# Last stage of a graph kernel: the scalar edge attribute moved into a second one-hot, edge weights formed two pairs ahead, ScalarE without its products of the weights

## What is computed

```python
tpw = h @ W_mlp4 / sqrt(64)
w1, w2, w3, w4 = split(tpw, 4)                 # 128 each
p1 = w1 * s0 * y0
p2 = (w2 * s0)[:, :, None] * y1[:, None, :]
p3 = w3[:, :, None] * s1 * y0[:, None, :]
p4 = w4 * einsum('eum,em->eu', s1, y1) / sqrt(3)
msg0 = segment_sum(concat(p1, p4), receiver)   # target node
msg1 = segment_sum(concat(p2, p3), receiver)
out = x1 + linear(msg0, msg1) / 10             # x1: the node features before this layer
```

## Time and profile before

| | |
|---|---|
| runs | 5696.2, 5701.41, 5704.77 us |
| profiled execution | 5664.33 us, span 5662.4 us |
| mean granted TensorE clock | 0.938 of full; 0.99 from 3191 us on |
| TensorE busy | 4809.4 us (85%), weight loads 2243.0 |
| VectorE busy | 2867.7 us (51%) |
| ScalarE busy | 2291.3 us (40%) |
| GpSimd busy | 2726.7 us (48%) |
| last stage, 3191 to 5663 us | TensorE 2279.0, VectorE 1782.5, ScalarE 1547.9, GpSimd 928.7 us busy |

### The profile page before, as it was taken

The page is one execution under the profiler, slowest core; times in us unless marked ns, Lnnn a source line. Parts: engine busy times, 40 slices in busy tenths (PEclk is TensorE's granted clock), DMA queues, the critical chain, the costliest instruction groups (busy, mean ns, idle before and its releaser), DMA issues.

```text
span 5662.4 us, 106923 instructions
## 1 busy us (share of the span) xinstructions
PE 4809.4 (85%) x17040; PEld 2243.0 (40%) x17041; DVE 2867.7 (51%) x8231; ACT 2291.3 (40%) x6164; POOL 2726.7 (48%) x3492
## 2 busy tenths in 40 slices
PE   7898566778898878887788899999999999998998
PEld 5443122333343223333344444444444444444444
DVE  7543122334453111123344577777777777777676
ACT  0442000111112223431223466666666666666565
POOL 0333666776664655456666344433333333333332
PEclk9998677899998889998899999999999999999999
DMA  2233666777776767667777444444433343333333
GB/s 83 95 106 112 178 191 205 222 227 234 238 246 191 214 207 220 195 208 236 249 254 267 148 119 115 116 116 118 120 112 115 117 120 113 115 117 113 113 117 95
DMA packets 433675, 916.83 MB, mean 162 GB/s; under 512 B 63093, under 2 KB 170869, under 8 KB 433510
## 3 DMA queue, kind: packets, MB, share of 16 engines
q0 software_dynamic: 195840, 641.89, 38.0%
q1 hardware_dynamic: 182918, 245.65, 13.0%
q10 hardware_dynamic: 54880, 28.91, 1.7%
HBM read 787.79 MB, written 128.41 MB: 162 GB/s over the span
## 4 chain that ended last, share of the span: by engine, by line
PE 30%; issue 24%; DVE 11%; DVEq 8%; ACT 7%; ACTq 7%; POOL 4%; DMA 3%; another core or an unknown queue 3%; POOLq 2%; SPq 0%
PE bank L1267 8%; POOL ring L544 4%; PE bank L1392 3%; PE bank L1223 3%; PE bank L1225 3%; ACT hB L788 3%; ACTq L785 3%; ACT dense_w L799 3%; DVEq L1110 2%; DVE hA L1118 2%; DVE hA L1104 2%; DVEq L1120 2%; DMA ef<-in_ef_t_dram 2%; PE bank L1310 2%
## 5 line engine op out<-in xcount | busy, mean ns | idle before, releaser
L544 POOL DMA_INDIRECT ring<-tab_d,idx x1568 | 1549.7, 988 | 817.4 <-issue 523.2
L1392 PE MATMUL bank<-dense_w,oh 128*128 128x512 f32 x3520 | 1618.6, 602 | 71.2 <-DVE dense_w L1127 70.3
L1267 PE MATMUL bank<-ring,ohp 128*128 x3904 | 1105.4, 436 | 462.0 <-POOLq L556 226.2
L510 POOL DMA_INDIRECT ring<-up_d,idx x880 | 856.7, 973 | 498.5 <-POOL idx L506 348.4
L799 ACT ACTIVATE dense_w<-hA,hC 128x128 f32<-128x128 f32 x2640 | 820.0, 389 | 664.4 <-DVE hA L1118 599.5
L1392 PEld LDWEIGHTS bank<-dense_w,oh 128*128 128x128 f32 x3520 | 632.8, 189 | 863.0 <-issue 666.7
L1267 PEld LDWEIGHTS bank<-ring,ohp 128*128 x3904 | 411.3, 107 | 1134.2 <-issue 866.0
L1015 DVE TENSOR_TENSOR ohp<-iota_w,dst_f 128x512 f32 x392 | 266.5, 692 | 679.8 <-PE bank L1267 246.3
L506 POOL COPY idx<-src_i 128x2 int32 x440 | 80.5, 183 | 1054.3 <-DVE dense_w L1127 1012.2
L1382 PE MATMUL bank<-w,hC 64*128 64x256 f32 x3520 | 504.6, 404 | 31.5 <-issue 20.9
L1104 DVE SCALAR_TENSOR_TENSOR hA<-ring,hC,hB 128x128 f32<-128x128 f32 x880 | 270.9, 349 | 500.9 <-ACT hB L788 436.6
(11 more groups left out here) (180 smaller groups left out, 4917.6 us busy)
## 6 DMA issues: line engine op xcount, KB each, us to landing
hC<-hid_d SPq DMA_DIRECT2D x440, 64.0 KB
tab_d<-tout SPq DMA_DIRECT2D x98, 256.0 KB, 2.8
tw<-tab_d SPq DMA_DIRECT2D x98, 256.0 KB
hlw<-hl_d SPq DMA_DIRECT2D x98, 256.0 KB
ring<-tab_d,idx POOLq DMA_INDIRECT x1568
hid_d<-hC ACTq DMA_DIRECT2D x98, 256.0 KB
hl_d<-agg SPq DMA_DIRECT2D x74, 256.0 KB, 3.1
ring<-up_d,idx POOLq DMA_INDIRECT x880
```

The costliest lines, as they stand in the source:

```text
L510: g_.indirect_dma_start(ring_v[:, b, k, :], None, table, bass.IndirectOffsetOnAxis(idx_t[:, b, k:k + 1], 0)).then_inc(S["got"][b], 16)
L544: g_.indirect_dma_start(ring_h[:, b, k, :], None, table, bass.IndirectOffsetOnAxis(idx_b[:, b, k:k + 1], 0)).then_inc(S["got"][b], 16)
L1267: ins = pe.matmul(bank[0][:, :], ohp_b[:, bass.ds(at, 1), k, :].rearrange("p b n -> p (b n)"), ring_b[:, bass.ds(slot, 1), k, h, :].rearra ...
L1392: ins = pe.matmul(bank[h][:, :], oh[:, b, k, :], msg[:, b, k, h, :], start=False, stop=False, skip_group_check=True)
```

## The change

- y0 is no longer multiplied into the weights. The one-hot for h = 0 is a second one, `oh0`, whose entries are y0 in place of 1: one `tensor_scalar` per tile with two operations (equal, then times y0), both with a scalar operand from memory. ScalarE's w13 products (L793) go, with their semaphores `w13` and `w_read`.
- The weights are two products of 512 columns per pair, into two adjacent banks, and there are two sets of these banks. The weights of pair n + 2 follow the sums of pair n.
- VectorE's order in a pair becomes: one-hot, t2 (one instruction for both tiles), p1 (one for both), wait for q0, q1, drain, q2, p3 (read from PSUM), the two weighted one-hots, drain, p4 (one for both). t2 has two buffers.
- The closing touches go; the copies of banks 0 and 1 wait for the last sum's `seg_done`. The second pair of a window is taken out of the loop, and the copy to `mT` comes behind it; the output product comes after the window's second sum.
- A window has at least `MINV` = 4 pairs in place of 2.

```diff
-        bank = [ctx.enter_context(nc.psum_tensor(f"bank{i}", [P, D], F32)) for i in range(8)]
+        ps = ctx.enter_context(nc.psum_tensor("bank", [P, 8, D], F32))
+        bank = [ps[:, i, :] for i in range(8)]
...
-        w_bank = [[bank[2], bank[3]], [bank[7], bank[5]]]
-        m_bank = [bank[4], bank[6]]
+        w_bank = [ps[:, 2:4, :], ps[:, 4:6, :]]
+        m_bank = [bank[6], bank[7]]
...
 weigh (ScalarE):
-                    ac.wait_ge(M["w_done"], n + 2)
-                    ac.wait_ge(M["u_used"], n + (NU - 1))
-                    for k in range(2):
-                        ins = ac.mul(w13[:, k, :], w_bank[k][0][:, 0:2 * P], yg[:, b, 4 * k:4 * k + 1])
-                    ins.then_inc(M["w13"], 1)
...
 messages (VectorE):
+                    w = w_bank[b]
+                    ve.wait_ge(M["seg_done"], n)
+                    ve.tensor_tensor(oh[:, b, :, :], iota_w[:, :].unsqueeze(1).broadcast_to([P, 2, P]),
+                                     dst_f[:, bass.ds(g * 2, 2)].unsqueeze(2).broadcast_to([P, 2, P]), ALU.is_equal)
+                    ve.wait_ge(M["got"][ub], ve.snap((n + (NU - 1)) // NU * 32))
+                    ve.wait_ge(M["w_done"], n + 2)
+                    ve.tensor_tensor(t2[:, b, :, :], w[:, :, 2 * P:3 * P], u[:, :, 0:P], ALU.mult).then_inc(M["t2"], 1)
+                    ve.tensor_tensor(msg[:, b, :, 0, 0:P], w[:, :, 0:P], u[:, :, 0:P], ALU.mult)
                     ve.wait_ge(M["q0"], n)
                     (q1, two instructions, as before)
-                    ve.wait_ge(M["seg_done"], n)
-                    (the one-hot)
                     ve.drain()
                     (q2, two instructions, as before)
-                    (t2, drain, p4, wait for w13, p1 and p3: eight instructions)
+                    for k in range(2):
+                        ve.tensor_tensor(msg[:, b, k, 0, P:].rearrange("p (m u) -> p m u", m=3),
+                                         w[:, k, P:2 * P].unsqueeze(1).broadcast_to([P, 3, P]),
+                                         u[:, k, P:4 * P].rearrange("p (m u) -> p m u", m=3), ALU.mult)
+                    for k in range(2):
+                        ve.tensor_scalar(oh0[:, b, k, :], iota_w[:, :], dst_f[:, bass.ds(g * 2 + k, 1)],
+                                         yg[:, b, 4 * k:4 * k + 1], ALU.is_equal, ALU.mult)
+                    ve.drain()
+                    ve.tensor_tensor(msg[:, b, :, 1, 0:P], q2[:, :, :], w[:, :, 3 * P:4 * P], ALU.mult).then_inc(M["u_used"], 1)
...
 window (ScalarE and VectorE; finish on VectorE only):
+                second_pair(w)
+                if not isinstance(w, int) or w > 0:
+                    copy_mT(w - 1)
                 rest(w)
                 if not isinstance(w, int) or w > 0:
                     finish(w - 1)
                 if not isinstance(w, int) or w < NW - 1:
                     first_pair(w + 1)
                 keep_b(w)
-                copy_mT(w)
...
 edge_weights and sum_pair (TensorE):
-                pe.wait_ge(M["w_read"], n)
-                pe.wait_ge(M["w13"], n)
-                for h in range(2):
-                    for k in range(2):
-                        ins = pe.matmul(w_bank[k][h][:, 0:2 * P], hid[k * HID:(k + 1) * HID, b, :],
-                                        w4[k * HID:(k + 1) * HID, h * 2 * P:(h + 1) * 2 * P], start=True, stop=True)
+                if not isinstance(n, int):
+                    pe.wait_ge(M["u_used"], n + (NU - 2))
+                for k in range(2):
+                    ins = pe.matmul(w_bank[b][:, k, :], hid[k * HID:(k + 1) * HID, b, :],
+                                    w4[k * HID:(k + 1) * HID, :], start=True, stop=True)
...
-                        ins = pe.matmul(bank[h][:, :], oh[:, b, k, :], msg[:, b, k, h, :], start=False, stop=False,
-                                        skip_group_check=True)
+                        ins = pe.matmul(bank[h][:, :], (oh0, oh)[h][:, b, k, :], msg[:, b, k, h, :], start=False,
+                                        stop=(last and k == 1), skip_group_check=True)
...
 the loop (TensorE):
+                def one(b):
+                    sum_pair(n, b, last)
+                    if ahead:
+                        edge_weights(n + 2, b)
...
+                step(True)
+                if not isinstance(w, int) or w < NW - 1:
+                    step(True)
+                    if not isinstance(w, int) or w > 0:
+                        out_product(w - 1)
+                    with pe.Fori(lo + 2, hi - 1) as g:
+                        step(True)
+                    step(True, True)
...
-                touch(bank[0][:, :], D, False)
-                touch(bank[1][:, :], D, False).then_inc(M["sum_done"], 1)
```

More of the change, by code:

```diff
@@ L32 @@
 LAG = 1
+MINV = 4
 NU = 4
@@ L176, in build @@
         yg = hC[:, 1, 0:16].rearrange("p (b n) -> p b n", b=2)
-        w13 = hA[:, 0, :].rearrange("p (k n) -> p k n", k=2)
-        t2, q1 = (hA[:, 1, i * 256:(i + 1) * 256].rearrange("p (k n) -> p k n", k=2) for i in range(2))
+        t2 = hA[:, 0, :].rearrange("p (b k n) -> p b k n", b=2, k=2)
+        q1 = hA[:, 1, 0:256].rearrange("p (k n) -> p k n", k=2)
+        oh0 = yb[:, :].rearrange("p (b k n) -> p b k n", b=2, k=2)
         q2 = hB[:, 0, 0:256].rearrange("p (k n) -> p k n", k=2)
@@ L809, in first_pair, with second_pair @@
                 weigh(lo)
+            def second_pair(w):
+                weigh(ac.snap(lo_r) + 1)
             def rest(w):
-                with ac.Fori(ac.snap(lo_r) + 1, ac.snap(hi_r)) as g:
+                with ac.Fori(ac.snap(lo_r) + 2, ac.snap(hi_r)) as g:
                     weigh(g)
             def keep_a(w):
-                ac.wait_ge(M["sum_done"], w + 1)
+                more = 1 if isinstance(w, int) and w == NW - 1 else 0
+                ac.wait_ge(M["seg_done"], ac.snap(c) + more)
                 after(ac, M["turned"], w)
@@ L893, in _ @@
             ve.drain()
-            ve.tensor_scalar(rcol[:, 0:1], rcol[:, 6:7], float(NG - 2), None, ALU.min)
+            ve.tensor_scalar(rcol[:, 0:1], rcol[:, 6:7], float(NG - MINV), None, ALU.min)
             ve.tensor_reduce(rcol[:, 5:6], rtmp2[:, :], X, ALU.max)
             ve.drain()
-            ve.scalar_tensor_tensor(out=rcol[:, 1:2], in0=rcol[:, 0:1], scalar=2.0, in1=rcol[:, 5:6],
+            ve.scalar_tensor_tensor(out=rcol[:, 1:2], in0=rcol[:, 0:1], scalar=float(MINV), in1=rcol[:, 5:6],
                                     op0=ALU.add, op1=ALU.max)
@@ L1138, in first_pair, with second_pair @@
                 messages(lo)
+            def second_pair(w):
+                messages(ve.snap(lo_r) + 1)
             def rest(w):
-                with ve.Fori(ve.snap(lo_r) + 1, ve.snap(hi_r)) as g:
+                with ve.Fori(ve.snap(lo_r) + 2, ve.snap(hi_r)) as g:
                     messages(g)
@@ L1147, in keep_b @@
             def keep_b(w):
-                ve.wait_ge(M["sum_done"], w + 1)
+                more = 1 if isinstance(w, int) and w == NW - 1 else 0
+                ve.wait_ge(M["seg_done"], ve.snap(c) + more)
                 after(ve, M["turned"], w)
@@ L1178, in _ @@
             over_windows(ve, window)
+            copy_mT(NW - 1)
             finish(NW - 1)
@@ L1417, in out_product, with step @@
                 ins.then_inc(M["o_done"], 1)
-            def weights_ahead():
+            def step(ahead, last=False):
                 n = pe.snap(c)
-                def step(b):
-                    edge_weights(n, b)
-                    sum_pair(n - 1, 1 - b)
-                pick(pe, pe.snap(n % 2), 0, 2, step)
+                def one(b):
+                    sum_pair(n, b, last)
+                    if ahead:
+                        edge_weights(n + 2, b)
+                pick(pe, pe.snap(n % 2), 0, 2, one)
                 pe.reg_add(c, c, 1)
```

50 lines of the change are left out of this document (16 added, 34 removed).

## The result

The changed kernel takes **5918.88 us** (median of 4 runs, 5913.02 to 5931.91) against 5703.09 in the same session: ratio 1.0382, 95% interval 1.0361 to 1.0403. It is slower by 216 us, where 18 less than the 5701 of then were forecast, and lies outside the range of 5600 to 5785. The profiled execution took 5918.87 us, its span is 5917.1.

The account below looks back on a forecast made before the run. VectorE and ScalarE waiting for each other were taken as the bound; 439 pairs at 5.29 us plus 48 edges at 2.3 gave 2432 against 2450, 18 less than the 5701 median: 5683 us, range 5600 to 5785.

Parts of the forecast that it names:

- the ring: Last stage: VectorE and ScalarE wait for each other once a pair, round trip 4.92 us; the new order breaks this.
- TensorE's four weight passes: TensorE, each pair: four passes of double length cost the same 1.13 us as eight old ones, or 0.43 more if unpaired.
- VectorE's exposed turn: VectorE's sequencer between pairs: 1.5 us from the last product's start to the next one-hot, bounds 0.34 and 1.6.
- The sums' wait for VectorE: TensorE's sums waiting for VectorE: grows to about 0.6 us a pair, a sign that the forecast is right.
- The first interval at an edge: VectorE at a window edge: the first pair ends 7.0 us after the last pair's end.
- Window edge: Between windows: second interval 5.6 us (copy and turn 1.4, pair 4.2); extra per edge 2.3 us against 5.7 before.
- D: Rival: VectorE's pair above 5.45 us for another cause, second memory scalar or slower loop bodies; 5770 us, chance 0.07.
- The engine's part of a pair: VectorE's engine time from the pair's start to the start of its last product: 3.79 us.
- the weighted one-hot: VectorE's tensor_scalar with two memory scalars: 0.29 us to its end, from a 0.287 row; bounds 0.23 and 0.35.
- the 0.3 at the third: Window edge: output product and turned copy stand behind the second pair and add 0.3 us.
- Rival C's collision: VectorE's weighted one-hots collide with GpSimd's gathers: 0.12 us each, 105 us more, 5788 us; chance 0.14.

Follow-up runs that it names:

- small: Changed kernel with VectorE's second pair back in the loop over pairs, the copy to mT following under a once-a-window condition; 5727.91 us, ratio 1.02 to the kernel before.
- small3_reorder: small2_reorder with the copy of the second half of the sums moved from VectorE to ScalarE; 5427.92 us, ratio 0.967 to the kernel before.
- small2: Changed kernel with VectorE's second pair back in the loop without a condition, its copy to mT moved to ScalarE; 5650.95 us, ratio 1.0066 to the kernel before.
- small2_reorder: small2 with VectorE's weighted one-hots ahead of the first drain and the wide messages last in a pair; 5535.32 us, ratio 0.986 to the kernel before.
- both shifts: Changed kernel with 128 or 256 idle instructions ahead of VectorE's last stage; 5834.56 and 5844.05 us, ratios 1.0402 and 1.0406 to the kernel before.
- before_peel2: Kernel before with the second and third pair of a window ahead of VectorE's loop, work order unchanged; 5850.87 us, ratio 1.0438.
- before_peel: Kernel before with only the second pair of a window ahead of VectorE's loop, work order unchanged; 5608.73 us, ratio 0.9996.

## Why the prediction was wrong

**Where it held.** That the ring opens and q0 is waited for no more: shown. That TensorE's four weight passes take as long as the eight did: yes,

```profile
4370.66 1.13 PE L1388 MATMUL bank<-w,hC 64*128 64x512 f32 x4
```

That the gain of the open ring goes into VectorE's exposed turn: yes, 1.55 us in the mean of the four bodies ((3 x 1.68 + 1.15) / 4) for 1.5. The sums' wait for VectorE came out at 0.4 us a pair (171.0 us in all) where 0.6 was named. The first interval at an edge 7.14 for 7.0. And small shows that the edge's new order gives the second interval that was read from the trace, 5.82 for 5.6.

**The step that failed** is "Window edge", its "then copy and turn, 1.4, and the second pair 4.2: 5.6". The turn was priced from rows of a kernel whose code stays loaded. In the changed kernel it holds one or two code fetches of about 2.9 us in 45 of 49 windows: 9.46 measured, and 49 x 3.86 = 189 us of the 228 that separate the measured 2660 from the forecast 2432. No rival had it, though D named "slower loop bodies": the prediction counted the work that moved and not the code that was added. Taking the second pair out of a loop was costed as a change of order, with nothing for its code and no reason given; it also wrote four more bodies of a pair into a loop that runs 46 times.

**Terms that were mis-sized.** The engine's part of a pair is 3.82 for 3.79, the turn 1.55 for 1.5, and the weighted one-hot 338 ns for 287 (the upper bound, 0.35, was nearer). Over 342 intervals with the 0.3 at the third: 1853 us for 342 x 5.29 + 48 x 0.3 = 1824, 29 us too few, and the first intervals were 7 us too few. These two alone would have given about 5719 and a time inside the range. Rival C's collision did not come: 880 weighted one-hots between 328 and 344 ns.

```profile
L1128 DVE TENSOR_SCALAR yb<-iota_w,dst_f,hC x880: 328/338/344, 3239.5 to 5899.7; 128x128 f32<-128x128 f32 x176
```

In the faster versions it does appear, here in small3_reorder, where the mean is 380 ns. All 309 that took over 350 ns ran beside GpSimd's gather (L513), but so did 407 that took their usual time. What it costs that kernel was not tried:

```profile
L1121 DVE TENSOR_SCALAR yb<-iota_w,dst_f,hC x880: 329/341/500, 3141.2 to 5408.6; 128x128 f32<-128x128 f32 x176
```

**The clock** is not the cause of the long second interval: it is lower in small too (0.926 over the run, 0.92 in the changed kernel), where that interval is 5.82. TensorE does run part of the stage at the lower of its two levels, 1.2 in place of 2.4 GHz, each time after it has been idle at an edge: in the changed kernel a transposed copy's product takes 417 ns in the median against 272 in small3_reorder. There it costs nothing that can be seen, since VectorE's own stall is longer. In small2 and small2_reorder, without stalls, it costs some 1.5 us in each window where it falls, at the third interval. The prediction had no term for it. No run held the clock by itself.

```profile
L1410 PE MATMUL bank<-ident,agg x196: 271/417/421, 3546.0 to 5905.6; 128*128 128x128 f32 x196
```

```profile
L1394 PE MATMUL bank<-ident,agg x196: 271/272/300, 3416.1 to 5417.5; 128*128 128x128 f32 x196
```

**What stays open.** The limit is known only as between 264 and 297 instructions, waits and drains not counted (306 and 322 with them), for a loop of this form on VectorE. Whether the loop's place against the packets' borders shifts it was not tried, since both shifts were whole packets. Why the number of packets (238 in the stage, five to a window) is what it is, and why each gap has its length, was not tried either. ScalarE's window code grew from 159 to 212 and has no stall, which fits the same limit.

## What to carry to other kernels

Code is a resource of an engine: before a pair is taken out of a loop whose body is written out per buffer, count the instructions between the outer loop's branch and its target on each engine, and compare the packets of the instruction queue of the two pages; 27 against 258 is visible at once. A drain ahead of the last instruction of a body left only that instruction's 0.42 us to cover the sequencer's turn, here 1.55 us; put queued, independent work behind it. With both mended, and the edge's copies on the engine with room, the kernel is 3.3% faster than the one before; as the change stood it cost 3.8%. How much of the 3.3% the moved copies would give the kernel before by themselves was not tried.

## What the runs showed of the hardware

- A loop over windows on VectorE with 180, 195 or 264 counted instructions runs without fetches (27 to 30 packets in the whole run); with 294, 297 or 348 it fetches each time the loop starts again: 257, 258 and 303 packets of 8 KB, and gaps of 2.1 to 4.7 us behind a branch. In these runs it is a step and not a slope: 84 instructions more cost 0 us, the next 84 cost 244.
- A packet of the instruction queue, 8 KB, holds 128 instructions: 128 more brought one more, twice. Shifting the loop by one or two packets changes nothing in the time (ratio 1.0402 and 1.0406 for 1.0382). The Trainium skill, Runtime: NRT & Kernel Launch, section Instruction fetch mechanics, says that a taken branch whose target is not in the two pages of code that are held forces a fetch before execution goes on. The gaps behind L306 and L297 agree with that rule. Its figure of 512 instructions for what is held, in blocks of 256, does not give the limit seen, between 306 and 322 instructions with waits and drains, nor would a loop of 327 instructions, waits and drains counted, then pass over a shift of half a block, since it could touch three blocks in at most one of the two places. The same section says that kernels prefer full unrolling; in before_peel2 one pair more written out than in before_peel cost 4.4%.
- TensorE's granted clock fell to the lower level at the opening of a window in 29 of 49 windows of small2_reorder, after it had been idle for about 2.5 us there, and in these the third interval took 7.35 us for 5.78. In small3_reorder, where its wait at that place is half as long (60.8 us in all for 120.6), it did not fall at any.
- A tensor_scalar with two scalars from memory takes 338 ns for 128 elements, with one 287 and with none 227.
